# Another written-out order for L2's last group, F2 and L3's prologue: L3's first weight tiles behind the gates' copies

## The reference

```python
x = x + jnp.tanh(g_xattn[2]) * _L2_xattn_ref(_layernorm(x), ctx_4096, ctx_4096, pos, mask, Wq, Wk, Wv, Wo)
x = x + jnp.tanh(g_ffn[2])   * _L2_ffn_ref(_layernorm(x), W_base, b_base, W_router, lora_A, lora_B)
x = x + jnp.tanh(g_xattn[3]) * _L3_xattn_ref(_layernorm(x), ctx_4096, ctx_4096, Wq, Wk, Wv, Wd)
```

```python
probs = softmax(xf @ W_router.T); topk_p, topk_i = top_k(probs, 2)
h = einsum('td,erd->ter', xf, lora_A)
out = x @ W_base.T + b_base + einsum('ter,eor,te->to', h, lora_B, w) * 2
```

## Time and profile before

| | before |
|---|---|
| median of 3 runs | 1801.08 us |
| the profiled execution | 1802.1 us |
| its span, first to last instruction | 1800.3 us |
| PE busy | 1754.0 us, 97% |
| DVE, ACT, POOL busy | 1213.5, 859.0, 969.2 us |
| share of PE in the chain that ended last | 91% |
| mean granted clock of PE | 0.993 |

### The profile page before, as it was taken

How to read it: one execution, slowest core, us unless ns; L and a number is a source line. 1 busy time by engine, 2 the same in 40 slices (tenths; PEclk the granted TensorE clock), 3 DMA queues, 4 the chain that set the end, 5 groups by cost and what they waited for, 6 DMA issues and landing times.

```text
span 1800.3 us, 27501 instructions
## 1 busy us (share of the span) xinstructions
PE 1754.0 (97%) x8776; PEld 1438.7 (80%) x8776; DVE 1213.5 (67%) x2204; ACT 859.0 (48%) x2451; POOL 969.2 (54%) x806
## 2 busy tenths in 40 slices
PE   4999999999999999999999999999999999999999
PEld 3788888776878888888888877878888888888887
DVE  5566566688876666666666675766666666666685
ACT  4466666553554444444444453344444444444451
POOL 3032322266575656656566563575675756757561
PEclk9999999999999999999999998999999999999999
DMA  5010100020111101101011110110110101101101
GB/s 208 6 34 21 30 24 16 21 91 12 59 42 30 47 12 52 35 29 47 17 51 36 29 34 25 41 48 19 51 35 23 47 24 46 36 22 47 31 18 48
DMA packets 36853, 69.47 MB, mean 39 GB/s; under 512 B 4362, under 2 KB 5130, under 8 KB 36658
## 3 DMA queue, kind: packets, MB, share of 16 engines
q1 hardware_dynamic: 36786, 68.61, 12.6%
HBM read 66.50 MB, written 2.10 MB: 38 GB/s over the span
## 4 chain that ended last, share of the span: by engine, by line
PE 91%; DVE 4%; issue 2%; ACT 2%; POOL 1%; DMA 1%; SPq 0%; POOLq 0%; ACTq 0%; DVEq 0%
PE ps L440 27%; PE ps L442 26%; PE ps L441 26%; PE ps L671 4%; PE ps L652 3%; PE ps L582 1%; PE ps L613 1%; DVE negmax L1522 1%; DMA bthr<-in_b_thr 0%; POOL probs L3268 0%; POOL rope_a L3250 0%; DVE pt_loL L1544 0%; DVE ot_lo L1555 0%; ACT probs L2518 0%; DVE ot_lo L1550 0%
## 5 line engine op out<-in xcount | busy, mean ns | idle before, releaser
L3268 POOL TENSOR_TENSOR probs<-probs,rsums 128x512 f32<-128x512 f32 (+1 forms) x160 | 194.8, 1218 | 281.4 <-DVE rsums L1540 281.2
L3250 POOL TENSOR_TENSOR rope_a<-rope_a,rope_b 128x512 f32<-128x512 f32 x160 | 206.9, 1293 | 155.0 <-DVE rope_b L1515 154.8
L440 PE MATMUL ps<-wo_hiL,ot_hi 128*128 128x512 f32 x608 | 248.8, 409 | 3.0 <-DVE ot_lo L1555 2.2
L440 PE MATMUL ps<-xt_hi,wq_hiL 128*128 128x512 f32 x608 | 242.6, 399 | 0.2
L442 PE MATMUL ps<-wo_hiL,ot_lo 128*128 128x512 f32 x608 | 241.5, 397 | 0.0
L441 PE MATMUL ps<-wo_loL,ot_hi 128*128 128x512 f32 x608 | 241.3, 397 | 0.0
L442 PE MATMUL ps<-xt_hi,wq_loL 128*128 128x512 f32 x608 | 238.0, 391 | 0.0
L441 PE MATMUL ps<-xt_lo,wq_hiL 128*128 128x512 f32 x608 | 236.9, 390 | 0.0
L2518 ACT ACTIVATE probs<-ps,negmax 128x128 f32<-128x128 f32 x512 | 182.1, 373 | 88.3 <-DVE negmax L1522 88.2
L2535 ACT CAST ot_hi<-ps 128x512 fp32r<-128x512 f32 (+1 forms) x160 | 90.7, 567 | 257.0 <-PE ps L442 256.6
L3262 POOL TENSOR_TENSOR q_loL<-rope_a,q_hiL 128x512 fp32r<-128x512 f32 x128 | 164.5, 1294 | 28.1 <-ACT q_hiL L2505 28.1
(11 more groups left out here) (231 smaller groups left out, 4267.0 us busy)
## 6 DMA issues: line engine op xcount, KB each, us to landing
raw<-in_L_proj SPq DMA_DIRECT2D x108, 256.0 KB, 2.6
raw<-in_L_out SPq DMA_DIRECT2D x76, 256.0 KB, 2.6
raw<-in_F_w SPq DMA_DIRECT2D x16, 256.0 KB, 2.7
x<-in_x SPq DMA_DIRECT2D x8, 256.0 KB, 4.3
ct_raw<-in_ctx_t SPq DMA_DIRECT2D x4, 512.0 KB, 7.6
cn_raw<-in_ctx SPq DMA_DIRECT2D x8, 256.0 KB, 8.1
out<-x SPq DMA_DIRECT2D x8, 256.0 KB, 2.0
raw<-in_L_kv SPq DMA_DIRECT2D x6, 256.0 KB, 2.9
```

Of the source, the lines that this page charges most:

```text
L440: pe.matmul(dst, l_hi, r_hi, start=start, stop=False)
L3250: gp.tensor_tensor(rope_a[:, a], rope_a[:, a], rope_b[:], ALU.add).then_inc(L.s_rsum, 1)
L3268: gp.tensor_tensor(pv, pv, rsums[:, b % 2].unsqueeze(2).to_broadcast([P, GH, L.keys]), ALU.mult).then_inc(L.s_p, 1)
```

## The change

Only the four written-out orders of `middle` change. No instruction is added or taken away, SP's order of DMAs is the same, and no helper changes. On ACT, F2's base tiles 1 to 3 go behind `pt_head(7)`, and L3's first two weight tiles, which stood ahead of and behind `o_head(6)` and `pt_head(7)`, go behind the copies of F2's first gates; on POOL the expert tile and L3's first weight tiles go ahead of the last norms; on PE the norm transposes of F2 come earlier and gates 4 to 7 of F2 stand together behind the first three experts.

PE:

```diff
 
 middle(a2, a3):
 last = Lq[1].groups - 1
+a2.keys_queries(1, last)
 a2.scores(0, last)
-a2.keys_queries(1, last)
 a2.fillers(0, last, only=0)
 a2.keys_queries(2, last)
 a2.scores(1, last)
+a2.fillers(0, last, only=1)
+a2.keys_queries(3, last)
+a2.scores(2, last)
 a2.transposes(0, last)
-a2.fillers(0, last, only=1)
-a2.scores(2, last)
-a2.keys_queries(3, last)
-a2.heads_out(0, last)
 a2.fillers(1, last, only=0)
 a2.fillers(1, last, only=1)
+a2.heads_out(0, last)
 a2.transposes(1, last)
 a2.fillers(2, last, only=0)
 a2.out_proj(0, last)
...
 a2.keys_queries(4, last)
 a2.heads_out(2, last)
 a2.transposes(3, last)
+a2.scores(4, last)
 a2.keys_queries(5, last)
-a2.scores(4, last)
 a2.out_proj(2, last)
 a2.heads_out(3, last)
+a2.keys_queries(6, last)
 a2.scores(5, last)
+pe.wait_ge(Lq[1].s_rope, Lq[1].ready("KQ", last, 1))
+pe.wait_ge(Lq[1].s_v, Lq[1].ready("V", last, 1))
+norm_transpose("F2", 0)
 a2.transposes(4, last)
-a2.keys_queries(6, last)
 a2.out_proj(3, last)
 a2.heads_out(4, last)
 a2.scores(6, last)
...
 a2.transposes(5, last)
 a2.out_proj(4, last)
 a2.heads_out(5, last)
-pe.wait_ge(Lq[1].s_rope, Lq[1].ready("KQ", last, 1))
-pe.wait_ge(Lq[1].s_v, Lq[1].ready("V", last, 1))
-norm_transpose("F2", 0)
 a2.scores(7, last)
 a2.transposes(6, last)
 norm_transpose("F2", 1)
+norm_transpose("F2", 2)
 a2.out_proj(5, last)
 a2.heads_out(6, last)
-norm_transpose("F2", 2)
+norm_transpose("F2", 3)
 a2.transposes(7, last)
 gates(2, 0)
 a2.out_proj(6, last)
-norm_transpose("F2", 3)
 gates(2, 1)
 a2.heads_out(7, last)
+norm_transpose("F2", 4)
 gates(2, 2)
-norm_transpose("F2", 4)
+norm_transpose("F2", 5)
 gates(2, 3)
 a2.out_proj(7, last)
-norm_transpose("F2", 5)
 products(2, 0)
 norm_transpose("F2", 6)
-gates(2, 4)
 products(2, 1)
 turn(2, 0)
 products(2, 2)
 experts(2, 0)
 experts(2, 1)
+experts(2, 2)
+norm_transpose("F2", 7)
+gates(2, 4)
 gates(2, 5)
-norm_transpose("F2", 7)
-experts(2, 2)
 gates(2, 6)
 gates(2, 7)
 products(2, 3)
 experts(2, 3)
-norm_transpose("A3", 0)
 pe.wait_ge(f_tdone, FQ[2] + 1)
 a3.begin(3, 0)
 products(2, 4)
+norm_transpose("A3", 0)
 turn(2, 1)
 products(2, 5)
 experts(2, 4)
+experts(2, 5)
 norm_transpose("A3", 1)
 pe.wait_ge(f_tdone, FQ[2] + 2)
 a3.begin(4, 1)
 norm_transpose("A3", 2)
-experts(2, 5)
 norm_transpose("A3", 3)
 products(2, 6)
+experts(2, 6)
 a3.begin(5, 0)
-experts(2, 6)
 a3.begin(3, 1)
 products(2, 7)
 experts(2, 7)
```

DVE, cut in two places:

```diff
 a2.row_max(0, last)
 a2.masked(1, last)
 a2.row_sum(0, last)
+a2.evacuate(0, 0, last)
+a2.row_max(1, last)
+a2.masked(2, last)
+a2.row_sum(1, last)
+a2.masked(3, last)
+a2.pt_tail(0, last)
+a2.row_max(2, last)
 scale_bias(2)
-a2.evacuate(0, 0, last)
-a2.pt_tail(0, last)
-a2.masked(2, last)
-a2.row_max(1, last)
-a2.masked(3, last)
-a2.row_max(2, last)
-a2.row_sum(1, last)
-a2.ot_tail(0, last)
 a2.evacuate(1, 0, last)
 a2.evacuate(1, 1, last)
+a2.ot_tail(0, last)
+a2.pt_tail(1, last)
 a2.row_sum(2, last)
-a2.pt_tail(1, last)
 a2.evacuate(2, 0, last)
...
 a2.row_max(6, last)
-norm_rows("F2", 1)
+a2.masked(7, last)
+norm_rows("F2", 2)
 a2.pt_tail(5, last)
+a2.row_sum(6, last)
 a2.next_stats(3, last)
-a2.row_sum(6, last)
-a2.masked(7, last)
 a2.residual(4, last)
 a2.ot_tail(5, last)
 a2.row_max(7, last)
+norm_rows("F2", 3)
 a2.pt_tail(6, last)
-norm_rows("F2", 2)
 a2.row_sum(7, last)
-norm_tail("F2", 0)
+norm_tail("F2", 1)
 a2.residual(5, last)
+a2.next_stats(4, last)
 a2.ot_tail(6, last)
-norm_rows("F2", 3)
-norm_tail("F2", 1)
-a2.next_stats(4, last)
+a2.next_stats(5, last)
+a2.pt_tail(7, last)
 norm_tail("F2", 2)
-a2.pt_tail(7, last)
 norm_rows("F2", 4)
 a2.residual(6, last)
 norm_tail("F2", 3)
-a2.next_stats(5, last)
+norm_rows("F2", 5)
+a2.next_stats(6, last)
 a2.ot_tail(7, last)
-a2.next_stats(6, last)
 norm_tail("F2", 4)
-norm_rows("F2", 5)
+norm_tail("F2", 5)
 logits(2, 0)
+norm_rows("F2", 6)
+top2_gate(2, 0, 0)
+top2_gate(2, 0, 1)
 a2.residual(7, last)
-top2_gate(2, 0, 0)
-norm_rows("F2", 6)
-top2_gate(2, 0, 1)
-norm_tail("F2", 5)
 top2_gate(2, 0, 2)
+top2_gate(2, 0, 3)
 norm_tail("F2", 6)
-top2_gate(2, 0, 3)
 weigh(2, 0)
 a2.next_stats(7, last)
 turned(2, 0)
+norm_rows("F2", 7)
 residual(2, 0)
-norm_rows("F2", 7)
 residual(2, 1)
+residual(2, 2)
 next_stats("A3", f_x, 0, FN[2])
+next_stats("A3", f_x, 1, FN[2])
 norm_tail("F2", 7)
-residual(2, 2)
...
```

ACT:

```diff
 a2.wo_head(2, last)
 a2.exps(0, last)
 a2.head(7, 1, last, BEFORE)
+a2.exps(1, last)
+a2.head(0, 1, last)
+a2.head(0, 0, last)
 a2.pt_head(0, last)
 a2.wo_head(3, last)
-a2.head(0, 1, last)
-a2.exps(1, last)
 a2.head(1, 0, last)
+a2.pt_head(1, last)
 a2.o_head(0, last)
 a2.exps(2, last)
-a2.head(0, 0, last)
-a2.pt_head(1, last)
 a2.head(1, 1, last)
 a2.o_head(1, last)
-a2.pt_head(2, last)
-a2.head(2, 0, last)
 a2.last_read(last)
 gate_weight(2)
+a2.head(2, 0, last)
+a2.pt_head(2, last)
 a2.exps(3, last)
-a2.base_weight(0)
-a2.base_weight(1)
 a2.o_head(2, last)
 a2.pt_head(3, last)
 a2.exps(4, last)
 a2.o_head(3, last)
-a2.base_weight(2)
+a2.base_weight(0)
 a2.pt_head(4, last)
-a2.base_weight(3)
 a2.exps(5, last)
+norm_head("F2", 0)
 a2.o_head(4, last)
 a2.pt_head(5, last)
 a2.exps(6, last)
 a2.o_head(5, last)
-norm_head("F2", 0)
 a2.pt_head(6, last)
 norm_head("F2", 1)
 a2.exps(7, last)
-expert_weight(2)
-a3.weights(0)
 a2.o_head(6, last)
 a2.pt_head(7, last)
-a3.weights(1)
+a2.base_weight(1)
+norm_head("F2", 2)
+a2.base_weight(2)
+a2.base_weight(3)
+norm_head("F2", 3)
 taken(2, 0)
-norm_head("F2", 2)
 taken(2, 1)
-norm_head("F2", 3)
 a2.o_head(7, last)
 norm_head("F2", 4)
+expert_weight(2)
 taken(2, 2)
+norm_head("F2", 5)
+a3.weights(0)
 taken(2, 3)
+a3.weights(1)
 gate_exps(2, 0)
 a3.weights(2)
-norm_head("F2", 5)
 norm_head("F2", 6)
 turned(2, 0)
 taken(2, 4)
+norm_head("F2", 7)
+a3.weights(3)
 taken(2, 5)
-norm_head("F2", 7)
 taken(2, 6)
+norm_rows("A3", 0)
+norm_rows("A3", 1)
 taken(2, 7)
-a3.weights(3)
-norm_rows("A3", 0)
 gate_exps(2, 1)
-norm_rows("A3", 1)
+turned(2, 1)
 norm_rows("A3", 2)
 norm_head("A3", 0)
-turned(2, 1)
+norm_head("A3", 1)
 a3.weights(4)
-a3.weights(5)
 norm_rows("A3", 3)
-norm_head("A3", 1)
-a3.begin(3, 0)
 a3.begin(4, 1)
 norm_head("A3", 2)
 norm_head("A3", 3)
+norm_rows("A3", 4)
+a3.weights(5)
+a3.begin(3, 0)
 a3.begin(5, 0)
-norm_rows("A3", 4)
+a3.begin(3, 1)
 norm_rows("A3", 5)
-a3.begin(3, 1)
 norm_head("A3", 4)
 norm_rows("A3", 6)
 a3.begin(4, 0)
+norm_rows("A3", 7)
 norm_head("A3", 5)
 norm_head("A3", 6)
-norm_rows("A3", 7)
 a3.begin(5, 1)
 norm_head("A3", 7)
 a3.begin(6, 0)
```

POOL:

```diff
 middle(a2, a3):
 last = Lq[1].groups - 1
 a2.add_up(7, 1, last, BEFORE)
+a2.tail(7, 1, last, BEFORE)
+a2.normalise(0, last)
+a2.add_up(0, 0, last)
 a2.wo_tail(0, last)
-a2.wo_tail(1, last)
-a2.normalise(0, last)
-a2.wo_tail(2, last)
-a2.add_up(0, 0, last)
-a2.wo_tail(3, last)
-a2.tail(7, 1, last, BEFORE)
 a2.normalise(1, last)
 a2.tail(0, 0, last)
+a2.wo_tail(1, last)
+a2.wo_tail(2, last)
+a2.wo_tail(3, last)
 a2.add_up(1, 1, last)
 a2.normalise(2, last)
+a2.tail(1, 1, last)
 a2.add_up(2, 0, last)
-a2.tail(1, 1, last)
+gate_weight(2)
 a2.tail(2, 0, last)
 norm_rstd("F2", 0)
 a2.normalise(3, last)
+norm_rstd("F2", 1)
+a2.normalise(4, last)
 add_bias(2, 0)
-gate_weight(2)
-a2.normalise(4, last)
-a2.normalise(5, last)
-norm_rstd("F2", 1)
-a2.base_weight(0)
 add_bias(2, 1)
 norm_rstd("F2", 2)
+a2.normalise(5, last)
 a2.normalise(6, last)
+a2.base_weight(0)
+norm_rstd("F2", 3)
 a2.normalise(7, last)
-norm_rstd("F2", 3)
 norm_rstd("F2", 4)
 a2.base_weight(1)
 a2.base_weight(2)
+norm_rstd("F2", 5)
 a2.base_weight(3)
+norm_rstd("F2", 6)
+expert_weight(2)
+norm_rstd("F2", 7)
+a3.weights(0)
 add_bias(2, 2)
-add_bias(2, 3)
-norm_rstd("F2", 5)
-norm_rstd("F2", 6)
-norm_rstd("F2", 7)
-expert_weight(2)
 norm_rstd("A3", 0)
-a3.weights(0)
 a3.weights(1)
 norm_rstd("A3", 1)
+a3.weights(2)
 norm_rstd("A3", 2)
-norm_rstd("A3", 3)
+add_bias(2, 3)
+a3.add_up(3, 0, 0, PROLOGUE)
 add_bias(2, 4)
 add_bias(2, 5)
-a3.weights(2)
 a3.weights(3)
-a3.add_up(3, 0, 0, PROLOGUE)
+norm_rstd("A3", 3)
+add_bias(2, 6)
 a3.weights(4)
-add_bias(2, 6)
+norm_rstd("A3", 4)
+a3.tail(3, 0, 0, PROLOGUE)
+norm_rstd("A3", 5)
 a3.weights(5)
 add_bias(2, 7)
-norm_rstd("A3", 4)
-a3.tail(3, 0, 0, PROLOGUE)
 a3.add_up(3, 1, 0, PROLOGUE)
-norm_rstd("A3", 5)
 norm_rstd("A3", 6)
+a3.tail(3, 1, 0, PROLOGUE)
 norm_rstd("A3", 7)
-a3.tail(3, 1, 0, PROLOGUE)
 a3.add_up(4, 0, 0, PROLOGUE)
 a3.tail(4, 0, 0, PROLOGUE)
 a3.add_up(5, 1, 0, PROLOGUE)
```

More of the change, by code:

```diff
@@ L1970, in middle @@
                 a2.row_max(3, last)
+                a2.next_stats(0, last)
                 a2.pt_tail(2, last)
-                a2.next_stats(0, last)
                 a2.row_sum(3, last)
@@ L1978, in middle @@
                 a2.row_max(4, last)
+                a2.next_stats(1, last)
                 a2.pt_tail(3, last)
-                a2.next_stats(1, last)
+                a2.masked(5, last)
+                norm_rows("F2", 1)
                 a2.row_sum(4, last)
-                a2.masked(5, last)
                 a2.residual(2, last)
                 a2.ot_tail(3, last)
+                a2.masked(6, last)
```

(40 more changed lines are left out.)

## The result

| | before | after |
|---|---|---|
| five runs taken together, median | 1800.58 us (1800.49 to 1801.22) | 1790.40 us (1787.90 to 1791.26) |
| ratio, 95% interval | | 0.9940 (0.9926 to 0.9953) |
| all runs of the study, median | 1800.9 us (73 runs, 1797.2 to 1804.5) | 1790.2 us (10 runs, 1786.9 to 1791.3) |
| profiled execution, its span | 1802.1, 1800.3 us | 1787.9, 1786.1 us |
| PE busy | 1754.0 us | 1745.9 us |

The change takes 10 to 11 us off. The direction and the mechanism were as forecast; the gain is 0.8 us (in the profile) to 1.3 us (in the medians) larger than the 9.4 forecast. In the profile the changed stretch, from the start of L2's last group to the wait for st in L3's first group, went from 1177.15 - 1044.09 = 133.06 us to 1163.26 - 1040.37 = 122.89, 10.17 less. What follows it is the same to 0.3 us (623.15 and 622.84).

What follows compares the result with a forecast made beforehand. PE bounds the kernel (busy 97%), so only its idle time and low clock can be won. Off 3.97 + 5.25 + 0.4 = 9.6, on 0.2, net 9.4: 1801.1 - 9.4 = 1791.7 us, range 1789.8 to 1795.3.

Steps and rivals of the forecast that it cites:

- The stall, 3.97: PE's single wait for pt_lo of L2's last batch, before heads_out(7): 3.97 us off, bounds 0 and 3.97.
- rival D: PE waits 2 to 4 us elsewhere in the norm chain, half the low clock returns: 1797 to 1801; chance 0.06.
- The half clock behind it, 5.25: PE's 11.17 us at half clock after the pt_lo wait become 5.92: 5.25 us off, other bound 0.
- `transposes(0)`, 0.4: PE's wait for POOL's normalised probs goes, as transposes(0) moves behind other PE work: 0.4 us off, 0 to 0.4.
- `gate_weight` and the gate chain, 0.1 and 0.1: Added waits at keys_queries(4) (0.1, bounds 0 to 1.3) and F2's turn (0.1, bounds 0 to 0.9).
- The waits that were to stay: 0.5 us at out_proj(1); 0.9 for st and the other 0.4 at the start of L3's first group.
- F3's wait for hw: Sign of being right: this 0.9 us wait in F3 would still be there.
- Rival B: Clock falls elsewhere, in F2's gates 4 to 7 run in one go: price 1.6 us, 1793.3; chance 0.08.
- Rival A: Several small new waits from the tighter order: price 1 to 3 us in all, 1792.8 to 1794.8; chance 0.18.
- Rival C: Stall moves with ACT's a3.weights(1) cast to the gate chain: 1.6 us slower, 1802.7; chance 0.04.
- its point of decision: Whether POOL's base_weight(1) ends more than 3 us before ACT reaches weights(1); forecast some 8 us before.

Runs made afterwards that it cites:

- act_one: Kernel before with ACT's cast a3.weights(1) moved from behind pt_head(7) to behind taken(2, 3); 1792.31 us, ratio 0.9949.
- pool_one: Kernel before with POOL's cast a2.base_weight(1) moved from behind norm_rstd("F2", 4) to behind normalise(7); 1792.29 us, ratio 0.9953.

## Where the prediction was right, and which step failed

The mechanism was right: one late tile, one wait, and a half clock behind it, and all of it goes. What failed is the price of the waits. I took each wait at its idle time, and that is too little; and I added 0.2 us for two new waits that never came.

- *The stall, 3.97.* The cause is right and shown from both ends (act_one takes the cast out of the way, pool_one brings the tile), and no other wait took its place, so rival D is out. The price is 4.13. act_one runs the same products as the kernel before, in the same order, so the two timelines of PE can be laid side by side. From the last product of `gates(2, 1)` to the first of `heads_out(7)` it is 1102.05 - 1097.81 = 4.24 us from start to start in the kernel before and 0.11 in act_one. Here are the rows of before, and then act_one's rows at the ends of the wait, of the 40 matmuls at half clock and of the out_proj:

```profile
1097.81 0.28 PE L442 MATMUL ps<-ag_hi,xt_lo 128*128 128x136 f32 x1
...
1113.99 0.60 PE L582 MATMUL ps<-consts,xn 128*128 128x128 f32 x4
```

```profile
1096.03 0.28 PE L442 MATMUL ps<-ag_hi,xt_lo 128*128 128x136 f32 x1
1096.14 0.45 PE L440 MATMUL ps<-pt_hiL,v_hiL 128*128 128x512 f32 x1
...
1102.08 0.40 PE L440 MATMUL ps<-wo_hiL,ot_hi 128*128 128x512 f32 x1
...
1102.78 0.60 PE L582 MATMUL ps<-consts,xn 128*128 128x128 f32 x4
```

- *The half clock behind it, 5.25.* Right. The 40 matmuls that took 11.17 us in the kernel before took 1102.08 - 1096.14 = 5.94 in act_one, where I had added up 5.92. Up to the norm transpose behind the out_proj (1113.99 in the kernel before) it is 11.94 against 6.64, a difference of 5.30. The Trainium skill (TensorE: Matmul & The Clock Gate, Terms) gives half of the throttled time, 5.6. This trace stays 0.3 below that: the same matmuls took 1.88 times as long at half clock, and not twice. What I missed is that the term isn't fixed: behind the same wait the price beyond it was 5.4 in one execution and 4.9 in another.
- *`transposes(0)`, 0.4.* The wait is gone, as forecast, and it too was worth more than its idle time. From `scores` to `transposes` PE takes 1047.92 - 1046.90 = 1.02 us in act_one, which still has the wait, and 1049.40 - 1048.97 = 0.43 in the kernel after: 0.59 for an idle time of 0.42.

```profile
1046.90 0.60 PE L652 MATMUL ps<-consts,st 128*128 128x128 f32 x4
1047.92 0.66 PE L671 MATMUL ps<-consts,probs 128*128 128x128 f32 x4 [0.42 <-POOL probs L3268]
```

```profile
1048.97 0.60 PE L652 MATMUL ps<-consts,st 128*128 128x128 f32 x4
1049.40 0.60 PE L671 MATMUL ps<-consts,probs 128*128 128x128 f32 x4
```

- *`gate_weight` and the gate chain, 0.1 and 0.1.* Neither wait came; there is no wait at `keys_queries(4)` or at the turn. The waits that were to stay stayed, and F3's wait for hw is 0.7 (0.9 in the earlier trace rows).
- *Sum for the stretch:* 4.13 + 5.30 + 0.59 = 10.02 of 10.17 measured; the other 0.15 lies in steps of less than 0.1 each. Against the 9.4 forecast the waits were priced 0.16 and 0.19 too low, the half clock 0.05, 0.2 was counted for nothing, and 0.15 was not in the sum. The median of 1790.4 is 1.3 below the forecast 1791.7, 0.5 more: the five runs of the kernel before now had their median at 1800.58 and not 1801.08, which is within what start-up and the low clock ahead of the stretch do to any kernel here.
- *Rival B, low clock in the run of gates 4 to 7:* no, in either profile of the kernel after. Rival A, small new waits: none. Rival C: its point of decision was passed by far; `base_weight(1)` ended on POOL at about 1090.8 and ACT reached `a3.weights(1)` at 1098.18, 7.4 us later (8 forecast).
- *The range.* The measured median lay only 0.6 us above its low end, and that is partly luck. The low end left 1.9 us for a gain larger than counted, of which the terms above took 0.8. I had read the spread off three runs of before that lay within 0.7 us; over 73 runs it is 7, and single executions of the kernel after reached 1786.9, well below the range.
